# A two-layer graph transformer on one core: layer 1 of a group runs one turn later, and its input is transposed by VectorE blocks and DRAM

## The chip, the core and the metric

The kernel runs on one NeuronCore of a Trainium2 chip. TensorE (PE in the profile, with PEld for its weight loads) multiplies matrices, VectorE (DVE), ScalarE (ACT) and GpSimd (POOL) work on elements, and the queue of SyncE (SP) issues all the large transfers. The metric is the device time of one execution in microseconds. Lower is better.

## The reference

`x` is 64 graphs of 128 nodes with 256 features in fp32, `adj` a 0/1 matrix of 128 x 128 for each graph. Two layers follow one another; a graph needs nothing of another graph.

```
# layer 0 (8 heads of 32)
nx = LN(x); q, k, v = nx@wq+bq, nx@wk+bk, nx@wv+bv
attn = softmax(q k^T / sqrt(32) + (adj > 0 ? 0.1*adj*adj : -inf))
x1 = x + (attn v)@wo + bo
x2 = x1 + gelu(LN(x1)@w1 + b1)@w2 + b2          # hidden 1024
# layer 1 (one head of 256)
s = (x2@Wq)(x2@Wk)^T / sqrt(256), -inf where adj == 0
y = x2 + softmax(s)@(x2@Wv)@Wo + bo1
out = LN(y)*gamma + beta
```

## The kernel before

**Groups and turns.** The 64 graphs are cut into 17 groups: group 0 and group 16 have two graphs, the others four (512 nodes). The work is a software pipeline written out by hand. Each engine has a function `turn` that lists its instructions for several groups in different phases, and turn `gp` is the one in which group `gp` has its Q, K, V and its scores. In that turn group `ga = gp-1` has its attention product, output projection and second LayerNorm, and group `gb = gp-2` has the whole MLP and then all of layer 1. VectorE and GpSimd also finish the last LayerNorm of group `gc = gp-3` and prepare the first one of group `gn = gp+1`. Groups 0 to 3 are started by `first_turn` and `second_turn`; turns 4 to 14 (to 15 on TensorE and ScalarE) are a hardware loop on each engine, the ones after are written out, and `last_turn` drains the pipe. Nothing is scheduled by a tool: the order on an engine is the order of the calls, and semaphores tie the engines together.

**Precision.** A product that needs fp32 accuracy is three passes in a faster format: a high part and a low part of each operand (`mm3`, lines 455 to 457). So each transposed activation has a ScalarE instruction that writes the high part and a VectorE instruction (`..._low`) that writes source minus high part.

**Names.** `mlp_up(g, j)` is one of eight tiles of the hidden layer; it waits for `h_low` of tile j-4, since four PSUM banks are shared. `mlp_down(g, q)` is the second MLP product of a pair of graphs. `residual2` adds it to `x1_b2` (x1 plus the bias b2) and gives `x2`. In layer 1, `t_project` is x2 times the folded Wq Wk^T, `scores1` the scores, `biased1` masks them and takes the row maximum, `exps1` the exponentials, `vo_project` x2 times the folded Wv Wo, `p1_transpose` and `attend1` the product with the probabilities, `residual3` gives `y`. `sums3`, `moments(3)`, `norm3` (VectorE) and `rstd`, `gain`, `offset` (GpSimd, lines 1920, 2004, 2009) are the last LayerNorm. In layer 0, `biased`, `exps`, `inverse`, `normal` and `blocks` make the probabilities of a pair of graphs, and `norm2` normalizes `x1` for the MLP.

**How x2 is transposed.** TensorE multiplies by the identity: `x2_transpose(gb)` (line 724) is eight 128x128 products into banks 4 and 5, `x2T_copy` and `x2T_high` on ScalarE write the fp32 copy and the high part, `x2T_low` on VectorE the low part. They sit in the middle of the turn, behind the second residual of the MLP. The input of layer 0 already takes another way: `xblocks` transposes 32x32 blocks on VectorE, SP stores them to DRAM (`store_nx`, four transfers) and loads them back in another order (`load_nx`), which completes the transpose; `nx_high` and `nxT_low` (line 1429) split what landed. The probabilities take that way too (`blocks`, `store_blocks`, `load_blocks`).

**The mask of layer 1.** GpSimd keeps a float copy of the adjacency one group behind: `move_up` (line 1968) copies `adj_g` to `adj_f`, `mask1` (line 1961) makes the penalty `pen1` of it.

**SP's queue** is one list in order; an issue behind one that waits, waits too.

Of the kernel before, what the change touches and what calls it, by code (L numbers as in the profile page):

```python
# [64 lines left out]
def build(nc, x, adj, ln1_g, ln1_b, ln2_g, ln2_b, wq, bq, wk, bk, wv, bv, wo, bo, w1, b1, w2, b2,  # L65
# [12 lines left out]
    with ExitStack() as ctx:  # L78
# [28 lines left out]
        probe = sb("probe", [128, 1])  # L107
# [6 lines left out]
        adj_f = sb("adj_f", [128, PER, NODES])  # L114
# [43 lines left out]
        parked_x = nc.dram_tensor("parked_x", (KT, 4, 32, NODES // 32, PER, 32), f32).ap()  # L158
        parked_end = nc.dram_tensor("parked_end", (KT, 4, 32, NODES // 32, 2, 32), f32).ap()
# [18 lines left out]

        def nx_split(part, g, t):
            return part[:, t, toks(g)].rearrange("p (b a i) -> p b a i", a=4, b=size(g))  # L180
# [6 lines left out]
        def home(n, g):  # L187
            return (own if is_last(g) else usual)[n]
# [36 lines left out]

        l1_bank, l1_mm_bank = (4, 6, 5), (7, 4)

        def at(n, g):
            if isinstance(g, int) and g < len(first_banks):
                return first_banks[g].get(n, usual_banks[n])  # L230
            return (own_banks if is_last(g) else usual_banks)[n]

# [56 lines left out]
        dve_blocks = sem("dve_blocks")  # L289
        dve_xblocks, nx_store, nx_load, xbo_load = sem("dve_xblocks"), sem("nx_store"), sem("nx_load"), sem("xbo_load")  # L290
# [32 lines left out]
        def _(sp):  # L323
# [38 lines left out]

            def store_blocks(g, q):
# [53 lines left out]
            def turn(gp, gc):  # L417
# [15 lines left out]
            with sp.Fori(3, GROUPS - 4) as g:  # L433
                turn(g + 1, g - 2)
            for g in range(GROUPS - 3, GROUPS):
                turn(g, g - 3)
            store(GROUPS - 3)
            for q in range(2):
                sp.wait_ge(dve_out, 2 * q + 2)
                sp.dma_start(out[graph0(GROUPS - 2) + 2 * q:graph0(GROUPS - 2) + 2 * q + 2].rearrange("b n d -> n b d"),  # L440
                             y[:, of_pair(q), :]).then_inc(out_store, 16)
# [7 lines left out]
        def _(pe):  # L449
# [132 lines left out]
            def project_v(g, q):  # L582
# [7 lines left out]
                elif not (isinstance(g, int) and g < 3):  # L590
                    pe.wait_ge(*((dve_x1, pair0(g) - 1), (dve_vo, g - 2))[q])
# [64 lines left out]
            def n2_transpose(g, B):  # L656
                if B:
                    pe.wait_ge(act_t, g)
                    pe.wait_ge(dve_t, g)
                    pe.wait_ge(dve_s1, g)  # L660
# [7 lines left out]
            def mlp_up(g, j, A):  # L668
# [78 lines left out]
            def vo_project(g, q, P):  # L747
                if isinstance(g, int) and g == 0:
                    pe.wait_ge(dve_lo, SPLIT["vo1"])
                if P and q == 0:  # L750
                    pe.wait_ge(act_v, pair0(g + 2) + 1)
                if P and q == 1:
                    pe.wait_ge(dve_x1, pair0(g + 1) + size(g + 1) // 2)
# [33 lines left out]
            def turn(gp, ga, gb):  # L787
# [9 lines left out]
                mlp_down(gb, 0)  # L797
                mlp_down(gb, 1, (0,))
                if size(gp) > 2:
                    scores(gp, 1)  # L800
                mlp_down(gb, 1, (1,))
# [12 lines left out]
                pe.wait_ge(act_vo, gb + 1)  # L814
                attend1(gb, 0)
                pe.wait_ge(dve_vo, gb)
                if size(gp) > 2:
                    pe.wait_ge(act_v, pair0(gp) + 2)
                attend1(gb, 1)
# [73 lines left out]
            def last_turn(ga, gb):  # L893

                for j in range(4):
                    mlp_up(gb, j, True)
                mlp_up(gb, 4, True)
                attend(ga, 0)
                mlp_up(gb, 5, True)
                mlp_up(gb, 6, True)  # L900
                out_project(ga, 0)
                mlp_up(gb, 7, True)
                mlp_down(gb, 0)
                n2_transpose(ga, False)
                mlp_down(gb, 1)
# [63 lines left out]
            with pe.Fori(3, GROUPS - 2) as g:  # L969
                turn(g + 1, g, g - 1)  # L970
            turn(GROUPS - 1, GROUPS - 2, GROUPS - 3)
            last_turn(GROUPS - 1, GROUPS - 2)


        @block.scalar
        def _(act):
# [111 lines left out]
            def x2T_copy(g, tiles=range(KT)):  # L1088
                for t in tiles:
                    act.wait_ge(pe_x2T, 2 * g + t + 1)  # L1090
                    identity(home("x2T_f", g)[:, t, toks(g)], bank[at("x2", g)[t]][:, toks(g)]).then_inc(act_x2T, 1)

            def x2T_high(g, tiles=range(KT)):
                for t in tiles:
                    act.wait_ge(act_x2T, 2 * g + t + 1)
                    identity(home("x2T", g)[0][:, t, toks(g)], home("x2T_f", g)[:, t, toks(g)]).then_inc(act_x2T_hi, 1)

            def last_x2T(g):

                for t in range(KT):  # L1100
                    act.wait_ge(pe_x2T, 2 * g + t + 1)
# [26 lines left out]
            def turn(gp, ga, gb):  # L1128
                whole = size(gp) > 2
                run(probe[:, :], minus_half[:, 0:1], ACT.Gelu)  # L1130
                nx_high(gp)
                for j in range(4):
# [6 lines left out]
                run(probe[:, :], minus_half[:, 0:1], ACT.Exp)  # L1139
# [6 lines left out]
                if whole:  # L1146
                    exps(gp, 1, 0)
# [999 lines left out]
```

## Time and profile before

| | us |
|---|---|
| time, median of 3 runs (890.16 to 891.61) | 890.98 |
| the profiled execution's own time | 891.15 |
| its span, first to last instruction | 889.4 |
| TensorE busy in the span | 853.3 (96%) |
| VectorE busy | 703.3 (79%) |
| ScalarE busy | 609.6 (69%) |
| GpSimd busy | 507.5 (57%) |
| transfers | 107.32 MB, 121 GB/s |

The span is what the rows below lie in; 1.75 us of the execution's own time lie around it. From turn 5 to turn 14 the turns are alike and one is about 50.9 us long. The time of a row is counted from the start of the span. The steady turn that the rows below show most of is turn 9: it ends where the next turn's first MLP product starts, at 473.44 us.

### The profile page before, as it was taken

The page shows a single profiled execution, that of the slowest core. Times are in us where ns is not written, and L with a number is a line of the kernel's source. Part 1 is how long each engine was busy: PE and PEld are TensorE (multiplying, and loading weights), DVE is VectorE, ACT ScalarE, POOL GpSimd, SP SyncE. Part 2 cuts the span into 40 slices and gives each one's busy share as a digit, 9 for nine tenths or more (in the row PEclk, how much of TensorE's full clock was granted, in tenths as well). Part 3 has the DMA queues.
Part 4 walks back from the last instruction along what each step waited for, and adds up shares of the span by engine and source line. Part 5 has one row for each costly group of instructions (what it writes and reads, how often), then busy time and mean ns, then how long its engine had stood idle before and what let it go on. Part 6 is the DMA issues. An engine that isn't in the chain of part 4 may idle for free.

```text
span 889.4 us, 21938 instructions
## 1 busy us (share of the span) xinstructions
PE 853.3 (96%) x7059; PEld 754.3 (85%) x7059; DVE 703.3 (79%) x2548; ACT 609.6 (69%) x1830; POOL 507.5 (57%) x374
## 2 busy tenths in 40 slices
PE   8899797799999999999999999999999999999996
PEld 8787687589898989889898988989798988989795
DVE  6695777868888898888888797888889887875636
ACT  5684865667868676776768676786867677684542
POOL 3522743756666565775647566666656577655312
PEclk9899999799999999999999999999999999999998
DMA  8000245445536353444546343553635343343001
GB/s 272 16 24 13 66 105 187 129 152 136 177 94 200 101 180 99 127 154 114 181 118 189 106 146 105 138 176 95 200 96 182 86 124 120 99 143 115 24 1 36
DMA packets 131122, 107.32 MB, mean 121 GB/s; under 512 B 5750, under 2 KB 112908, under 8 KB 131084
## 3 DMA queue, kind: packets, MB, share of 16 engines
q1 hardware_dynamic: 131068, 106.85, 40.5%
q8 instruction: 19, 0.31, 0.2%
q14 instruction: 19, 0.16, 0.1%
q10 hardware_dynamic: 16, 0.00, 0.0%
HBM read 61.48 MB, written 45.35 MB: 120 GB/s over the span
## 4 chain that ended last, share of the span: by engine, by line
PE 74%; ACT 3%; DVE 3%; POOL 1%; issue 1%; DVEq 0%; POOLq 0%
PE bank L455 21%; PE bank L457 20%; PE bank L456 20%; PE bank L618 3%; PE bank L743 3%; PE bank L774 3%; PE bank L642 3%; ACT p L1116 2%; PE bank L724 1%; DVE p L1540 1%; PE bank L767 0%; POOL p_s L2013 0%; POOL x_bo L1983 0%; POOL x_b L1993 0%; DVE stats L1375 0%
## 5 line engine op out<-in xcount | busy, mean ns | idle before, releaser
L1052 ACT ACTIVATE p_s<-bank,neg_max 128x128 f32<-128x128 f32 x464 | 163.0, 391 | 78.2 <-DVE neg_max L1443 78.1
L2013 POOL TENSOR_TENSOR p_s<-p_s,rsum 128x512 f32<-128x512 f32 x116 | 118.1, 1041 | 73.9 <-DVE rsum L1450 52.2
L455 PE MATMUL bank<-w_hi,hT_hi 128*128 128x256 f32 x512 | 147.5, 288 | 1.3 <-DVE hT_lo L1316 1.3
L457 PE MATMUL bank<-w_hi,hT_lo 128*128 128x256 f32 x512 | 144.1, 281 | 0.0
L456 PE MATMUL bank<-w_lo,hT_hi 128*128 128x256 f32 x512 | 144.0, 281 | 0.0
L1443 DVE CUSTOM_DVE_ANT_0 bank<-bank,bias 128x128 f32<-128x128 f32 x464 | 117.4, 325 | 2.0 <-PE bank L618 1.5
L455 PE MATMUL bank<-n2T_hi,w_hi 128*128 128x512 f32 (+1 forms) x272 | 111.4, 409 | 5.1 <-DVE hT_lo L1316 5.1
L1083 ACT ACTIVATE bank<-bank,vec_cols 128x512 f32<-128x512 f32 (+1 forms) x136 | 86.5, 636 | 31.1 <-PE bank L457 22.5
L1052 ACT ACTIVATION_READ_ACCUMULATOR p_s<-bank,neg_max 128x1 f32 x464 | 107.1, 231 | 0.0
L456 PE MATMUL bank<-n2T_lo,w_hi 128*128 128x512 f32 (+1 forms) x272 | 105.2, 387 | 0.0
L457 PE MATMUL bank<-n2T_hi,w_lo 128*128 128x512 f32 (+1 forms) x272 | 105.1, 387 | 0.0
L455 PEld LDWEIGHTS bank<-w_hi,hT_hi 128*128 128x128 f32 x512 | 96.3, 188 | 5.4 <-DVE hT_lo L1316 2.3
L1920 POOL TENSOR_TENSOR rstd<-ve,minus_half 128x4 f32<-128x4 f32 (+1 forms) x49 | 50.0, 1020 | 87.3 <-DVE ve L1385 85.8
L456 PEld LDWEIGHTS bank<-w_lo,hT_hi 128*128 128x128 f32 x512 | 96.4, 188 | 0.0
L457 PEld LDWEIGHTS bank<-w_hi,hT_lo 128*128 128x128 f32 x512 | 96.4, 188 | 0.0
L1316 DVE TENSOR_TENSOR hT_lo<-bank,hT_hi 128x512 fp32r<-128x512 f32 (+1 forms) x136 | 84.0, 647 | 10.7 <-ACT hT_hi L982 10.7
L1999 POOL TENSOR_TENSOR x<-x,bo_r 128x1024 f32<-128x1024 f32 (+1 forms) x16 | 37.4, 2338 | 94.8 <-PE bank L724 90.8
L982 ACT ACTIVATE hT_hi<-bank 128x512 fp32r<-128x512 f32 (+1 forms) x136 | 78.1, 574 | 5.3
L1466 DVE STREAM_TRANSPOSE pT<-p_s 128x512 f32<-128x512 f32 x116 | 78.5, 695 | 3.3 <-POOL p_s L2013 2.7
L455 PEld LDWEIGHTS bank<-n2T_hi,w_hi 128*128 128x128 f32 x272 | 52.4, 193 | 22.3 <-DVE hT_lo L1316 12.3
L1443 DVE DVE_READ_ACCUMULATOR2_ANT neg_max<- 128x1 f32 x512 | 68.1, 133 | 0.1
L457 PEld LDWEIGHTS bank<-n2T_hi,w_lo 128*128 128x128 f32 x272 | 52.2, 192 | 11.0
(242 smaller groups left out, 2432.6 us busy)
## 6 DMA issues: line engine op xcount, KB each, us to landing
parked<-pT SPq DMA_DIRECT2D x116, 256.0 KB, 3.8
pT<-parked SPq DMA_DIRECT2D x15, 1024.0 KB, 5.5
p_s<-parked SPq DMA_DIRECT2D x14, 1024.0 KB, 7.7
xs<-in_x SPq DMA_DIRECT2D x15, 512.0 KB, 3.9
out<-y SPq DMA_DIRECT2D x14, 512.0 KB, 3.0
x_bo<-in_x SPq DMA_DIRECT2D x13, 512.0 KB, 3.8
parked_x<-nx SPq DMA_DIRECT2D x48, 128.0 KB, 2.5
hT_hi<-parked_x SPq DMA_DIRECT2D x12, 512.0 KB, 5.0
```

What stands on the lines that cost most here:

```text
L455: mm(out, a_hi, b_hi, start=first, stop=False)
L456: mm(out, a_hi, b_lo, start=False, stop=False)
L457: return mm(out, a_lo, b_hi, start=False, stop=last)
L982: return run(dst, src, ACT.Identity, **kw)
L1052: last = run(to, of, ACT.Exp, scale=-1.0, bias=neg_max[:, r, place:place + 1], accum_out=psum[:, r, place:place + 1])
L1083: run(h, h, ACT.Gelu, bias=cols["b1"][:, j:j + 1]).then_inc(act_h, 1)
L1316: return V.tensor_tensor(dst, src, hi.bitcast(f32), ALU.subtract)
L1443: last = V.tensor_tensor_reduce(scored if by_blocks(g) else p_s[:, r, place, :], scored, bias0[:, 2 * q + place // 2, :], -1.0, -3.0 * MAS ...
L1466: V.transpose(pT[:, r, :, :].rearrange("p b (l i) -> p l b i", l=4), p_s[:, r, :, :].rearrange("p l (b j) -> p l b j", j=32)).then_inc(dve ...
L1920: P.tensor_tensor(t["rstd"][:, 0:k], t["ve"][:, 0:k], minus_half[:, 0:k], ALU.pow).then_inc(ln_pool[n], 1)
L1999: P.tensor_tensor(x[:, 0:k, :], x[:, 0:k, :], row_of("bo1", k), ALU.add).then_inc(pool_x2b, 1)
L2013: P.tensor_tensor(p_s[:, r, :, :], p_s[:, r, :, :], rsum[:, r, :, None].to_broadcast([128, 4, NODES]), ALU.mult).then_inc(pool_p, 1)
```

## The change

Layer 1 of a group moves one turn later, to group `gl = gp-3`, and the last LayerNorm with it, to `gc = gp-4`. This is so for groups 2 to 14 (`late(g)`); groups 0, 1, 15 and 16 keep TensorE's transposes. The parts:

- TensorE: no `x2_transpose` in the turns. Turn 4 has no layer 1 at all (`gl` is None); `last_turn` gets the layer 1 of group 14 between its MLP products.
- VectorE: `x2blocks(gb)` (two block transposes of x2 into `x1_b2`) stands where `x2T_low(gb)` stood; `x2T_low(gl)` now stands behind `norm3(gc)` and reads both its operands from SBUF.
- ScalarE: `landed_high(gl)` (two instructions) ahead of the turn's gelus, and the four instructions of `x2T_copy`/`x2T_high` gone.
- GpSimd: `mask_landed(gb)` makes the mask from an adjacency that is loaded again; `mask1` and `move_up` are gone. `x2_plus_bo(gb)` moves from between the two halves of the probabilities to behind the last of them.
- SP: in each turn four stores of 128 KB and one load of 512 KB for the transpose, a store and a load of 512 KB for x2 itself (it comes back in `y`, to be added in `residual3`), and a load of 256 KB for the adjacency.

The core of the diff:

```
+def late(g):
+    return not (isinstance(g, int) and (g < 2 or g > GROUPS - 3))
 # SP
-            def turn(gp, gc):
+            def turn(gp, gb, gl, gc):
...
                     load_adj(gp + 1)
-                store(gc)
+                load_adj1(gb)
+                if gc is not None:
+                    store(gc)
                 store_blocks(gp, 0)
+                if gl is not None:
+                    load_y(gl)
                 if not is_last(gp):
                     load_nx(gp + 1)
+                store_x2T(gb)
                 load_xbo(gp)
                 if not is_last(gp):
                     store_blocks(gp, 1)
+                load_x2T(gb)
                 for q in pairs(gp):
                     load_blocks(gp, q)
+                store_x2(gb)
 # TensorE
                 mlp_down(gb, 1, (1,))
                 out_project(ga, 0)
-                x2_transpose(gb)
                 out_project(ga, 1)
                 project_v(gp, 0)
-                t_project(gb)
-                vo_project(gb, 0, True)
-                scores1(gb)
-                vo_project(gb, 1, True)
+                t_project(gl)
+                vo_project(gl, 0, True)
+                scores1(gl)
+                vo_project(gl, 1, True)
                 n2_transpose(ga, True)
-                p1_transpose(gb)
+                p1_transpose(gl)
...
+            turn(4, 3, 2, None)
+            with pe.Fori(4, GROUPS - 2) as g:
+                turn(g + 1, g, g - 1, g - 2)
 # VectorE
+            def x2blocks(g):
+                dve.wait_ge(dve_x2, pair0(g) + 2)
+                turned = flat(x1_b2[:, :, :]).rearrange("p (t c b i) -> p t b c i", t=KT, c=4, b=PER)
+                for t in range(KT):
+                    V.transpose(turned[:, t], x2[:, :, 128 * t:128 * t + 128].rearrange(
+                        "p b (c j) -> p b c j", c=4)).then_inc(dve_x2blocks, 1)
...
+                    if late(g):
+                        V.tensor_tensor(nx_split(x2T[1], g, t), x2_landed(g, t), nx_split(x2T[0], g, t).bitcast(f32),
+                                        ALU.subtract).then_inc(dve_x2T, 1)
 # GpSimd
                 pool.wait_ge(ln_dve[2], ln_end(ga))
                 if size(gp) > 2:
                     normal(gp, 1, 3)
+                x2_plus_bo(gb)
                 x_plus_bo(gp)
                 x1_plus_b2(ga)
-                mask1(ga)
-                move_up(gp)
+                mask_landed(gb)
```

How the instructions stand on VectorE between the last LayerNorm and the scores' maxima, in the loop of the steady turns. `y` is the layer-1 output being normalized, `avT_lo` and `n2T_lo` the low parts that the output projection of group `ga` needs. Before:

```order
L1316 TENSOR_TENSOR hT_lo<-bank,hT_hi 128x512
L1392 TENSOR_SCALAR y<-y,mv,rstd 128x256 x4
L1478 REGISTER_ALU
L1316 TENSOR_TENSOR avT_lo<-bank,avT_hi 128x512
L1478 REGISTER_ALU
L1316 TENSOR_TENSOR n2T_lo<-bank,n2T_hi 128x512
```

Now:

```order
L1506 TENSOR_SCALAR y<-y,mv,rstd 128x256 x4
L1651 ISA
L1653 TENSOR_TENSOR x2T_lo<-x2T_f,x2T_hi 128x512
L1651 REGISTER_ALU
L1653 TENSOR_TENSOR x2T_lo<-x2T_f,x2T_hi 128x512
L1592 REGISTER_ALU
L1430 TENSOR_TENSOR avT_lo<-bank,avT_hi 128x512
```

Two instructions with both operands in SBUF have come between the LayerNorm and the low part of the attention output.

The end of GpSimd's steady turn, from the last probabilities (`p_s`) on; `x` is x2, `x_b` is `x1_b2`, `pen` the mask. Before:

```order
L2013 TENSOR_TENSOR p_s<-p_s,rsum 128x512
L1981 REGISTER_ALU
L1983 TENSOR_TENSOR x_bo<-x_bo,bo_r 128x1024
L1987 ISA
L1992 REGISTER_ALU
L1993 TENSOR_TENSOR x_b<-x,b_r 128x1024
L1961 TENSOR_SCALAR pen<-adj_f 128x512
L1968 COPY adj_f<-adj_g 128x512
```

Now:

```order
L2181 TENSOR_TENSOR p_s<-p_s,rsum 128x512
L2167 TENSOR_TENSOR x<-x,bo_r 128x1024
L2146 TENSOR_TENSOR x_bo<-x_bo,bo_r 128x1024
L2158 TENSOR_TENSOR x_b<-x,b_r 128x1024
L2121 CAST pen<-adj_w 128x512
L2124 TENSOR_SCALAR pen<-pen 128x512
```

The addition to x2 has moved in ahead of the three others, and the mask is now last.

## Rows read from the trace of the kernel before

**Rows 1.** Stretches: length, busy per engine, PEclk, DMA share, GB/s; turn 4, steady, last
```profile
160.61:219.07 58.46, 54.47 (x425) 47.52 (x424) 46.25 (x164) 39.04 (x122) 36.68 (x28) 0.92 0.47 135
...
483.63:534.49 50.86, 50.81 (x426) 44.80 (x425) 43.19 (x157) 36.99 (x111) 32.80 (x24) 1.00 0.47 139
...
825.00:876.50 51.50, 50.05 (x375) 45.57 (x374) 26.91 (x71) 25.65 (x57) 12.77 (x9) 1.00 0.03 11
```
**Rows 2.** Timeline, TensorE, second half of turn 9: start, length, what, idle before it
```profile
455.65 0.28 PE L455 MATMUL bank<-wo_hi,avT_hi 128*128 128x256 f32 x1
...
457.07 1.03 PE L724 MATMUL bank<-ident,x 128*128 128x128 f32 x8
457.86 0.36 PE L455 MATMUL bank<-wo_hi,n2T_hi 128*128 128x256 f32 x1
...
460.90 0.50 PE L455 MATMUL bank<-x2T_hi,qk_hi 128*128 128x512 f32 x1
...
463.78 0.28 PE L455 MATMUL bank<-vo_hi,x2T_hi 128*128 128x256 f32 x1
...
465.31 2.02 PE L743 MATMUL bank<-x2T_f,tT 128*128 128x128 f32 x16
...
468.74 1.09 PE L664 MATMUL bank<-ident,nx 128*128 128x128 f32 x8
469.66 0.90 PE L767 MATMUL bank<-ident,p 128*128 128x128 f32 x4
470.31 0.36 PE L455 MATMUL bank<-wv_hi,nxT_hi 128*128 128x256 f32 x1
...
471.81 1.98 PE L774 MATMUL bank<-vo,p1T 128*128 128x256 f32 x8
473.44 0.58 PE L455 MATMUL bank<-n2T_hi,w_hi 128*128 128x512 f32 x1
```
**Rows 3.** The same for VectorE in turn 9
```profile
438.77 1.38 DVE L1392 TENSOR_SCALAR y<-y,mv,rstd 128x256 f32<-128x256 f32 x4 [0.72 <-POOL rstd L1920]
441.73 0.69 DVE L1316 TENSOR_TENSOR avT_lo<-bank,avT_hi 128x512 fp32r<-128x512 f32 x1 [1.58 <-ACT avT_hi L982]
...
452.99 0.30 DVE L1443 CUSTOM_DVE_ANT_0 bank<-bank,bias 128x128 f32<-128x128 f32 x1 [0.15 <-PE bank L618]
...
464.52 0.65 DVE L1533 COPY tT<-bank 128x512 f32<-128x512 f32 x1
...
465.21 1.38 DVE L1392 TENSOR_SCALAR nx<-x,mv,rstd 128x256 f32<-128x256 f32 x4
...
474.67 1.75 DVE L1429 TENSOR_TENSOR nxT_lo<-hT_hi,nxT_hi 128x512 fp32r<-128x512 f32 x2
```
**Rows 4.** The same for ScalarE, end of the first pair's exponentials
```profile
449.73 0.30 ACT L1052 ACTIVATION_READ_ACCUMULATOR p_s<-bank,neg_max 128x1 f32 x1
```
**Rows 5.** The same for GpSimd
```profile
440.23 2.38 POOL L2004 TENSOR_TENSOR y<-y,gamma_r 128x1024 f32<-128x1024 f32 x1 [1.62 <-DVE y L1392]
...
467.75 2.38 POOL L1983 TENSOR_TENSOR x_bo<-x_bo,bo_r 128x1024 f32<-128x1024 f32 x1
...
472.57 1.94 POOL L1961 TENSOR_SCALAR pen<-adj_f 128x512 f32<-128x512 f32 x1
```
**Rows 6.** Timeline of GpSimd in the drain, an addition within SBUF
```profile
839.34 2.38 POOL L2009 TENSOR_TENSOR y<-y,beta_r 128x1024 f32<-128x1024 f32 x1
```
**Rows 7.** Timeline of VectorE at the same time
```profile
840.12 1.63 DVE L1385 TENSOR_SCALAR ve<-mv 128x2 f32<-128x2 f32 x1
```
**Rows 8.** Timeline of GpSimd, last instruction of its turn 10
```profile
525.57 1.17 POOL L1968 COPY adj_f<-adj_g 128x512 f32<-128x512 f32 x1 [0.16 <-issue]
```
**Rows 9.** Timeline of VectorE at the same time
```profile
525.57 1.71 DVE L1429 TENSOR_TENSOR nxT_lo<-hT_hi,nxT_hi 128x512 fp32r<-128x512 f32 x2
```
**Rows 10.** All instructions of line 1968: count, ns min/median/max, first and last start
```profile
L1968 POOL COPY adj_f<-adj_g x17: 397/612/1168, 12.4 to 823.7; 128x512 f32<-128x512 f32 x15, 128x256 f32<-128x256 f32 x2
```
**Rows 11.** Page, costliest groups: count, busy us, mean ns, idle before and releaser
```profile
L1466 DVE STREAM_TRANSPOSE pT<-p_s 128x512 f32<-128x512 f32 x116 | 78.5, 695 | 3.3 <-POOL p_s L2013 2.7
```

More of the change, by code:

```diff
@@ L891, in second_turn, with last_turn @@
                 attend1(1, 1)
-            def last_turn(ga, gb):
-                for j in range(4):
-                    mlp_up(gb, j, True)
+            def last_turn(ga, gb, gl):
+                mlp_up(gb, 0, True)
+                mlp_up(gb, 1, True)
+                t_project(gl)
+                mlp_up(gb, 2, True)
+                mlp_up(gb, 3, True)
+                scores1(gl)
+                vo_project(gl, 0, False)
+                attend(ga, 0)
                 mlp_up(gb, 4, True)
-                attend(ga, 0)
+                vo_project(gl, 1, False)
                 mlp_up(gb, 5, True)
                 mlp_up(gb, 6, True)
+                pe.wait_ge(dve_vo, gl)
                 out_project(ga, 0)
                 mlp_up(gb, 7, True)
+                p1_transpose(gl)
                 mlp_down(gb, 0)
+                attend1_pairs(gl)
+                mlp_down(gb, 1, (0,))
                 n2_transpose(ga, False)
-                mlp_down(gb, 1)
+                mlp_down(gb, 1, (1,))
                 for j in range(4):
@@ L1146, in turn @@
                 if whole:
[L1147 to L1154 removed]
+                    for r in range(HPT):
+                        exps(gp, 1, r)
                 v_copy(gp, 0)
[L1156 to L1158 removed]
+                if gl is not None:
+                    t_copy(gl)
+                    vo_copy(gl)
+                    exps1(gl)
                 n2T_copy(ga)
[L1160 removed]
+                if gl is not None:
+                    p1T_copy(gl)
                 if whole:
@@ L1233, in second_turn, with last_turn @@
                 exps(3, 1, 3)
-            def last_turn(ga, gb):
-                run(probe[:, :], minus_half[:, 0:1], ACT.Gelu)
+            def last_turn(ga, gb, gl):
+                run(probe[:, 0:1], minus_half[:, 0:1], ACT.Gelu)
+                landed_high(gl)
                 gelu(gb, 0)
                 gelu(gb, 1)
-                for j in range(2, 5):
-                    gelu(gb, j)
+                t_copy(gl)
+                gelu(gb, 2)
+                gelu(gb, 3)
+                vo_copy(gl)
                 attn_high(ga, 0)
-                for j in range(5, HT):
-                    gelu(gb, j)
+                gelu(gb, 4)
+                gelu(gb, 5)
+                run(probe[:, 1:2], minus_half[:, 0:1], ACT.Exp)
+                exps1(gl)
+                run(probe[:, 0:1], minus_half[:, 0:1], ACT.Gelu)
+                gelu(gb, 6)
+                gelu(gb, 7)
+                p1T_copy(gl)
                 n2T_copy(ga)
@@ L1630, in turn @@
                 h_low(gb, 7)
-                norm3(gc)
+                if gc is not None:
+                    norm3(gc)
+                if gl is not None:
+                    x2T_low(gl)
                 attn_low(ga, 0)
@@ L1663, in turn @@
                     blocks(gp, 1, 0)
-                t_copy(gb)
+                if gl is not None:
+                    t_copy(gl)
                 if whole:
@@ L1804, in last_turn @@
                 h_low(gb, 1)
+                t_copy(gl)
                 h_low(gb, 2)
+                norm3(gc)
+                h_low(gb, 3)
+                biased1(gl)
                 attn_low(ga, 0)
-                h_low(gb, 3)
-                norm3(gc)
+                vo_copy(gl)
+                h_low(gb, 4)
                 residual1(ga, 0, True)
-                h_low(gb, 4)
+                h_low(gb, 5)
                 sums2(ga, 0)
                 moments(2, ga)
-                h_low(gb, 5)
                 h_low(gb, 6)
@@ L2053, in second_turn @@
                 x1_plus_b2(2)
-                mask1(2)
-                move_up(3)
                 for r in range(HPT):
@@ L2065, in turn @@
                 bias(gp)
-                rstd(3, gc)
-                gain(gc, size(gc))
-                offset(gc, size(gc))
+                if gc is not None:
+                    rstd(3, gc)
+                    gain(gc, size(gc))
+                    offset(gc, size(gc))
                 for r in range(HPT):
                     normal(gp, 0, r)
-                x2_plus_bo(gb)
                 if size(gp) > 2:
@@ L2090, in last_turn @@
                 pool.wait_ge(ln_dve[2], ln_end(ga))
+                mask_landed(gb)
                 x1_plus_b2(ga)
+                rstd(3, gl)
                 x2_plus_bo(gb)
-                mask1(ga)
+                gain(gl, size(gl))
+                offset(gl, size(gl))
+                mask_landed(ga)
                 x2_plus_bo(ga)
```

256 lines of the change are left out of this document (177 added, 79 removed).

## The prediction

> **What bounds the kernel now.** First the chain of work that ended last, whose steps are TensorE's almost throughout. Then the stretches: in a steady turn of 50.86 us TensorE is busy for 50.81, VectorE for 43.19, GpSimd for 32.80 [rows 1]. So a steady turn is TensorE's list of instructions and nothing else; VectorE has 7.7 us left over. Turn 4 is different, 58.46 us with 54.47 busy at a granted clock of 0.92, that is partly at the lower of TensorE's two levels (1.2 instead of 2.4 GHz); the drain from 825.0 to 876.5 us is full again, 50.05 of 51.50 [rows 1]. Last, the timelines of turn 9: where each other engine stands against TensorE [rows 2 to 5].
>
> **What the transposes cost.** The eight stand from 457.07 us to the start of the next product at 457.86, and that one is followed more slowly for another 0.08: 0.87 us [rows 2]. Thirteen groups lose them. One wait of about 0.1 us ahead of `t_project` (460.90) goes too, so a turn that is bounded by TensorE gains 0.95.
>
> **What layer 1 costs, since it moves.** From [rows 2]: `t_project` 460.90 to 463.78, the first `vo_project` to 465.31, `scores1` and the second `vo_project` to 468.74, `p1_transpose` 469.66 to 470.31, `attend1` 471.81 to 473.44. That is 2.88 + 1.53 + 3.43 + 0.65 + 1.63 = 10.1 us of TensorE. Turn 4 loses it, `last_turn` gains it, turns 5 to 16 exchange one group's for another's.
>
> Term 1, the drain. There TensorE has 1.45 us of idle time in 51.5 [rows 1], so 10.1 us of work is nearly 10.1 us of time. The two waits that this idle time is made of do not go: ScalarE must now change its table for `exps1` and back between gelu 5 and gelu 6, which makes the last `h_low` of group 15 late by about as much as the wait that it replaces. **+10.1**, bounds +8.7 (all idle time filled) and +12 (table changes uncovered).
>
> Term 2, turn 4. It has 54.47 - 0.87 - 10.1 = 43.5 us of work left, but the second LayerNorm of group 3 does not come sooner. The end of `norm2` (465.21 + 1.38 = 466.59) is 10.9 us behind the end of the MLP, where the output projection starts (455.65) [rows 2, 3]; without `t_copy` (0.65), and with two block transposes (1.3) for what `x2T_low` and its waits took there (about 2.45), it is 9.1 to 9.3. In steady turns layer 1 fills this gap. In turn 4 only `project_v(gp, 0)` is left for it, 1.4 us, so TensorE stands for about 8 us ahead of `n2_transpose`. The two output projections (457.07 - 455.65 = 1.4 us each), which stood behind the last MLP product, stand before it now and put it off by 2.8. Summed, turn 5's first product comes 2 to 3 us sooner than at 219.07 us. But such an idle time lowers the granted clock (turn 4's 0.92), and the start of turn 5 then waits for VectorE (term 4 below), so at the seventh MLP tile of turn 5 I expect **+0.3**, bounds -3 (clock back soon) and +1. GpSimd's `mask1` and `move_up`, gone ahead of turn 4, save at most 0.9 of this, for the residuals on VectorE end nearly as late.
>
> **The steady turns: what the new places do.** The decisive view is how VectorE and GpSimd share SBUF. GpSimd runs one addition from 839.34 to 841.72; a VectorE instruction on four numbers, issued at 840.12, takes 1.63 us, to 841.75 [rows 6, 7]. At 525.57 both begin, GpSimd's copy and the two `nxT_low`: 1.71 us for the two and 1.17 for a copy whose median is 0.61 [rows 8 to 10]; I read this as VectorE's first, then the copy, then VectorE's second. So an instruction of VectorE with two SBUF operands, or a scaling within SBUF, excludes GpSimd's and waits for its whole length, and the two engines take turns. The low parts that read PSUM (`avT_lo`, 0.69) and the block transposes (mean 695 ns beside GpSimd's `normal`) do not show it [rows 3, 11].
>
> The Trainium skill says the same as a rule (GPSIMD Engine Reference, "1. Specifications"): GpSimd's SBUF interfaces are shared with VectorE, and contention arises with VectorE instructions in a 2-port mode or with two SBUF inputs. By that rule the moved `x2T_low`, which read PSUM before and reads SBUF twice now, speaks against this change; the trace above agrees. The page gives no price, the sum takes it from the rows.
>
> Term 3, `x2T_low` behind `norm3`. `norm3` ends at 440.15, and its end is what `gain` waits for: it starts at 440.23 and takes 2.38 [rows 3, 5]. VectorE's first half (0.6) gets in ahead, to 440.7; then `gain`, to 443.1; then the second half, to 443.7. `avT_lo`, which could start at 441.73, starts 1.9 us later, `n2T_lo` and `biased` (16 maxima) behind it about 1.7. ScalarE's exponentials of the first pair end at 450.03 [rows 4], now 451.75, and the second pair's scores on TensorE, at 451.59 before, wait 0.3. Behind them on VectorE stand the last `inverse`, `residual2`, three `blocks`, then the second `biased`: 454.55 instead of 452.99 [rows 3]. From there VectorE has no gap: the old order reached `t_copy`'s end at 465.17 [rows 3] with 2.45 for `x2T_low`; now 465.17 + 1.56 - 2.45 + 1.3 = 465.6. `scores1` waits for it: 465.7 instead of 465.31 [rows 2], though TensorE could be there at 464.6. That wait eats the transposes' gain. `norm2` ends 0.4 late, `biased1` and `exps1` 0.1 late, `attend1` ends 0.14 us later than before: **-0.95 turned into +0.14** per turn.
>
> Term 4, the start of the next turn. GpSimd goes on after `norm2` (467.05 now): `normal` 1.04, then three additions of 2.38 (before: two, from 467.75 [rows 5]), to 475.35; then the cast, like the copy 0.61 [rows 10], and the mask, 1.94 [rows 5]. `residual3` ends at 474.85, so `nxT_low` waits 0.5 for the last addition, then once more for the cast: 2.3 us for 1.75 [rows 3]. The small scaling ahead of `rstd` ends as the mask does, at 479.1. So `h_low` 0 to 3 come 0.6 to 0.75 later against `attend1`, and `h_low(3)` is what `mlp_up(7)` waits for already. **+0.6** per turn. ScalarE's 1.14 us for `landed_high` is hidden: it is busy for 36.99 of 50.86 us [rows 1], and `h_low(0)` waits for VectorE's own list, not for it. Bounds of terms 3 and 4 together: -0.95 (no collision costs anything) and +1.3 per turn.
>
> SP's queue. The stores of `store_x2T` (some 2 us of issuing) stand ahead of `load_xbo`, which is needed 6 us later; `load_x2T` stands ahead of `load_blocks`, which lands about 2 us later with 4 to 5 in hand. 0, and +1 per turn if that reserve is gone. The added 2.25 MB per turn of 51 us are 44 GB/s on 139 [rows 1].
>
> **The sum.** From turn 5's seventh tile to turn 15's are ten turns of +0.74: +7.4. Turn 16 has half of VectorE's work, so it keeps TensorE's gain: -0.95 + 0.14 = -0.8. With term 1, +10.1, and term 2, +0.3: +17.0 us on the profiled execution's 891.15, 908.2. It lies 0.17 above the median of the runs, so I forecast **908.0**, with its own range 901 to 915.
>
> **Rivals.**
> A. The engines do not collide there: VectorE's second half gets in ahead of `gain`, or the exclusion is shorter. Then the turns stay TensorE's: 10 x -0.8 (0.15 left for `nxT_low`) or -0.95, -0.95 in turn 16, +10.1 in the drain, -1.7 in turn 4 (clock back sooner). 891.15 - 9.5 - 0.95 + 10.1 - 1.7 = 889.1, or 891 with the smaller values. For it: VectorE's 7.7 spare us. Against: [rows 6 to 10]. It decides if `biased` starts no more than 0.8 us late. This is the case on the other side.
> B. `x2T_low` is late, but the second half of the turn takes it up, and each turn comes out even: 891.15 + 0 - 0.95 + 10.1 + 0.3 = 900.6.
> C. GpSimd's `gain` gets in first and `offset` before VectorE's second half: `biased` 2.4 us later still, 10 turns: 908 + 24 = 932. Against: `gain` waits for a semaphore of `norm3`, VectorE's next instruction does not. Or a transfer comes late, +1 per turn: 918.
>
> **Chances.** Forecast 0.62, A 0.17, B 0.12, C and beyond 0.09. A gain needs A with its better values (half of it), and a small rest: faster by over 0.2% (below 889.2) 0.09; within 0.2%, about what this measurement can tell from no change, 0.09; slower 0.82. The range takes in the upper part of A, B and the forecast's own bounds: 890 to 916.
>
> **What the changed profile would show.** Right: TensorE's busy share falls in steady turns and the turn grows to about 51.6; `scores1` is waited for by `tT`; the second `x2T_lo` of each turn takes some 3 us against 0.6 for the first; ScalarE waits longer for `neg_max`; an idle time of about 8 us ahead of `n2_transpose` near 205 us; the drain has layer 1 of group 14 with TensorE full. Wrong: two `x2T_lo` in 1.4 us, a turn of 50 us, or a turn 4 shorter by more than 5 us.

## The result, and the profile after

The changed kernel takes 929.84 us (927.9 to 931.08) against 891.22 before (890.16 to 891.61): ratio 1.0435, 95% interval 1.0422 to 1.0448. It is slower by 38.6 us where 17 were forecast, and outside the range (890 to 916). The profiled execution took 927.9 us, its span is 926.1.

The chain of waits of the page after, by engine and then by line, says at once that something new is in the path:

```profile
PE 61%; DVE 12%; DMA 8%; ACT 5%; issue 5%; SPq 4%; POOL 3%; DVEq 0%; POOLq 0%; ACTq 0%
PE bank L519 17%; PE bank L521 16%; PE bank L520 16%; DMA x2T_f<-parked_x2T 7%; SPq L418 4%; PE bank L708 3%; PE bank L684 3%; PE bank L824 3%; DVE pT L1580 2%; ACT bank L1183 1%; DVE hT_lo L1430 1%; DVE p L1668 1%; ACT hT_hi L1082 1%; ACT x2T_hi L1082 1%; DVE bank L1557 1%
```

New in it are a transfer, `x2T_f<-parked_x2T`, which is what `load_x2T` brings, and SP's line 418, which is `store_blocks`. Now the stretches, as in [rows 1] (length, busy per engine, granted clock, DMA share, GB/s). They are cut where the `attend1` of a turn ends. First the kernel before, from the end of turn 3: turns 4 and 5, turns 6 to 15, turn 16, `last_turn`.

```profile
160.70:270.31 109.61, 105.57 (x850) 92.57 (x849) 89.80 (x320) 76.29 (x233) 69.16 (x51) 0.96 0.47 137
270.31:779.03 508.72, 507.91 (x4241) 448.04 (x4241) 429.34 (x1555) 369.79 (x1111) 326.67 (x231) 1.00 0.46 136
779.03:825.32 46.29, 45.03 (x381) 41.03 (x381) 30.37 (x102) 29.47 (x80) 23.99 (x20) 1.00 0.38 121
825.32:889.40 64.08, 55.02 (x402) 49.15 (x401) 36.03 (x101) 27.33 (x63) 15.35 (x11) 0.96 0.06 21
```

And after, with turns 9 and 10 apart at the end:

```profile
157.59:267.81 110.22, 96.86 (x769) 85.03 (x769) 83.83 (x295) 70.00 (x217) 60.81 (x45) 0.92 0.55 161
267.81:800.67 532.86, 506.89 (x4161) 444.50 (x4161) 445.04 (x1575) 354.59 (x1091) 333.10 (x231) 0.98 0.60 174
800.67:850.71 50.04, 45.78 (x373) 41.13 (x373) 31.45 (x104) 28.39 (x80) 26.56 (x21) 0.97 0.57 165
850.71:926.10 75.39, 66.02 (x467) 59.69 (x465) 42.56 (x131) 33.96 (x79) 25.05 (x18) 0.95 0.14 47
428.15:481.88 53.73, 51.09 (x417) 44.95 (x417) 44.73 (x159) 35.53 (x110) 33.31 (x24) 0.97 0.60 176
481.88:534.51 52.63, 50.09 (x418) 43.68 (x417) 44.76 (x159) 35.32 (x110) 33.35 (x24) 1.00 0.62 179
```

Of the 36.7 us between the spans, +0.6 are in turns 4 and 5, +24.1 in turns 6 to 15, +3.8 in turn 16 and +11.3 in the drain; -3.1 lie ahead of turn 4. The last can't be put down to the change: over the eleven profiled kernels that share the changed kernel's code up to there that stretch ends anywhere from 157.2 to 160.7 us, and over the two with the code of before at 160.7 and 161.5. How much of it is scatter stays open, which is why turns are compared here and not starts.

So the drain is near the forecast and the steady turn is not: 53.3 us in the mean, not 51.6. In each turn TensorE has one large wait, of 2.3 to 2.7 us in turns 6 to 15. The start of turn 10 shows where it is from: first TensorE's `scores1`, the last reader of the old `x2T_f`, then SP's queue, ScalarE, VectorE with one line of GpSimd, and TensorE's fifth MLP tile (start, length, what, idle before it and who ended it).

```profile
473.46 1.95 PE L824 MATMUL bank<-x2T_f,tT 128*128 128x128 f32 x16
```

```profile
469.02 1.90 SPq L397 DMA_DIRECT2D parked_x2T<-x_b  x4
471.19 0.41 SPq L373 DMA_DIRECT2D x_bo<-in_x  x1
478.41 2.82 SPq L418 DMA_DIRECT2D parked<-pT  x4
481.48 0.92 SPq L404 DMA_DIRECT2D x2T_f<-parked_x2T  x1
```

```profile
482.12 1.14 ACT L1082 ACTIVATE nxT_hi<-hT_hi 128x512 fp32r<-128x512 f32 x2
486.58 1.15 ACT L1082 ACTIVATE x2T_hi<-x2T_f 128x512 fp32r<-128x512 f32 x2 [3.32 <-DMA x2T_f<-parked_x2T]
487.64 0.65 ACT L1183 ACTIVATE bank<-bank,vec_cols 128x512 f32<-128x512 f32 x1
488.40 0.60 ACT L1082 ACTIVATE hT_hi<-bank 128x512 fp32r<-128x512 f32 x1
```

```profile
477.69 0.69 DVE L1580 STREAM_TRANSPOSE pT<-p_s 128x512 f32<-128x512 f32 x1
...
482.76 0.60 POOL L2121 CAST pen<-adj_w 128x512 f32<-128x512 int32 x1
482.77 2.16 DVE L1543 TENSOR_TENSOR nxT_lo<-hT_hi,nxT_hi 128x512 fp32r<-128x512 f32 x2
...
489.03 0.69 DVE L1430 TENSOR_TENSOR hT_lo<-bank,hT_hi 128x512 fp32r<-128x512 f32 x1 [2.06 <-ACT hT_hi L1082]
```

```profile
489.78 0.50 PE L519 MATMUL bank<-n2T_hi,w_hi 128*128 128x512 f32 x1 [2.32 <-DVE hT_lo L1430]
```

The x2 blocks are stored at 469 to 471, `scores1` has read the old `x2T_f` at 475.41, and from then on the new one could be loaded. But `load_x2T` stands in SP's queue behind `store_blocks(gp, 1)`, which waits for VectorE's last block of the second pair (477.69 + 0.69 = 478.38) and then issues for 2.8 us. The load goes out at 481.48 and lands at 486.58. ScalarE has stood in `landed_high` since 483.26, ahead of all eight gelus; TensorE's fifth MLP tile waits for the first `h_low`. It happens in twelve turns: ScalarE waits 41.8 us in all, 3.3 to 3.7 in each of turns 6 to 15.

The collision that the forecast rests on is in the trace too, but the other way round. VectorE (first fence), then GpSimd:

```profile
502.08 1.29 DVE L1653 TENSOR_TENSOR x2T_lo<-x2T_f,x2T_hi 128x512 fp32r<-128x512 f32 x2
503.70 0.69 DVE L1430 TENSOR_TENSOR avT_lo<-bank,avT_hi 128x512 fp32r<-128x512 f32 x1 [0.33 <-ACT avT_hi L1082]
```

```profile
502.25 3.35 POOL L2172 TENSOR_TENSOR y<-y,gamma_r 128x1024 f32<-128x1024 f32 x1 [1.61 <-DVE y L1506]
```

Both halves of `x2T_low` get in (1.29 us for two), and it is `gain` that takes 3.35 us instead of the 2.38 of [rows 5]. It is so in the whole kernel: the median of the fifteen `gain` is 3.36 us here and 2.38 in experiment 2 below, where `x2T_low` stands elsewhere. VectorE loses nothing.

### The profile page after: what moved, and what is told of

Its sections match the earlier page's. It is cut to its first block, busy times and chain, and to the rows that moved or that the text cites. A ratio compares the mean times of both kernels' runs of the same rounds, so it can differ in the third digit from the quotient of the medians.

```text
span 926.1 us, 21993 instructions
## 1 busy us (share of the span) xinstructions
PE 852.5 (92%) x6955; PEld 751.5 (81%) x6955; DVE 720.5 (78%) x2574; ACT 593.7 (64%) x1808; POOL 517.2 (56%) x374
## 4 chain that ended last, share of the span: by engine, by line
PE 61%; DVE 12%; DMA 8%; ACT 5%; issue 5%; SPq 4%; POOL 3%; DVEq 0%; POOLq 0%; ACTq 0%
PE bank L519 17%; PE bank L521 16%; PE bank L520 16%; DMA x2T_f<-parked_x2T 7%; SPq L418 4%; PE bank L708 3%; PE bank L684 3%; PE bank L824 3%; DVE pT L1580 2%; ACT bank L1183 1%; DVE hT_lo L1430 1%; DVE p L1668 1%; ACT hT_hi L1082 1%; ACT x2T_hi L1082 1%; DVE bank L1557 1%
## 5 line engine op out<-in xcount | busy, mean ns | idle before, releaser
L519 PE MATMUL bank<-n2T_hi,w_hi 128*128 128x512 f32 (+1 forms) x272 | 116.0, 426 | 35.8 <-DVE hT_lo L1430 35.2
L1152 ACT ACTIVATION_READ_ACCUMULATOR p_s<-bank,neg_max 128x1 f32 x464 | 110.7, 239 | 0.0
L521 PE MATMUL bank<-n2T_hi,w_lo 128*128 128x512 f32 (+1 forms) x272 | 110.1, 405 | 0.0
L520 PE MATMUL bank<-n2T_lo,w_hi 128*128 128x512 f32 (+1 forms) x272 | 109.9, 404 | 0.0
L519 PEld LDWEIGHTS bank<-n2T_hi,w_hi 128*128 128x128 f32 x272 | 55.3, 203 | 56.8 <-DVE hT_lo L1430 45.8
L1557 DVE DVE_READ_ACCUMULATOR2_ANT neg_max<- 128x1 f32 x512 | 72.3, 141 | 0.1
L521 PEld LDWEIGHTS bank<-n2T_hi,w_lo 128*128 128x128 f32 x272 | 55.0, 202 | 12.0
L520 PEld LDWEIGHTS bank<-n2T_lo,w_hi 128*128 128x128 f32 x272 | 55.3, 203 | 10.8
```

Source lines behind the costliest of these rows:

```text
L519: mm(out, a_hi, b_hi, start=first, stop=False)
L520: mm(out, a_hi, b_lo, start=False, stop=False)
L521: return mm(out, a_lo, b_hi, start=False, stop=last)
L1152: last = run(to, of, ACT.Exp, scale=-1.0, bias=neg_max[:, r, place:place + 1], accum_out=psum[:, r, place:place + 1])
L1557: last = V.tensor_tensor_reduce(scored if by_blocks(g) else p_s[:, r, place, :], scored, bias0[:, 2 * q + place // 2, :], -1.0, -3.0 * MAS ...
```

## The experiments

Theory Q says that the load's place in the queue makes the loss of the steady turns, theory C that it is the collisions. All ratios are against the kernel before, run beside (889.3 to 889.8 us there).

**1. The load one place earlier.**

```diff
                 load_xbo(gp)
+                load_x2T(gb)
                 if not is_last(gp):
                     store_blocks(gp, 1)
-                load_x2T(gb)
```

> Edit: on SP, load_x2T stands ahead of store_blocks(gp, 1) instead of behind it, nothing else. In the changed kernel the load is issued at 481.48 us in turn 9, 3.1 us behind the end of the last block of the second pair (478.38), though its own two conditions hold from about 475.4 us; it lands at 486.58, and ScalarE, which stands in landed_high ahead of the gelus, waits 3.3 to 3.7 us for it in each of twelve turns. Theory Q (queue): the load's place in SP's queue makes nearly the whole loss of the steady turns. Then the load is issued at about 475.5, lands before ScalarE gets there, the wait of TensorE for hT_lo (2.3 to 2.7 us a turn) is mostly gone, a turn takes 50.6 to 51.2 instead of 53.3 us, the kernel 895 to 906 us. Theory C (collisions, my own of the prediction): VectorE and GpSimd in each other's way at x2T_low and nxT_low make the loss; then the turn stays above 52.5 and the kernel above 918 us.

Measured 889.1 us, ratio 0.9992 (0.9982 to 1.0003): 40 us from two lines that change places, and level with the kernel before. Its stretches, as above, and its turn 9 alone:

```profile
158.32:267.12 108.80, 96.02 (x770) 84.50 (x769) 84.00 (x294) 69.47 (x215) 60.49 (x45) 0.93 0.55 167
267.12:767.00 499.88, 497.19 (x4162) 437.66 (x4161) 444.89 (x1575) 354.36 (x1091) 333.05 (x231) 1.00 0.61 186
767.00:812.14 45.14, 43.88 (x374) 40.03 (x373) 31.32 (x104) 28.34 (x80) 26.59 (x21) 1.00 0.57 172
812.14:885.90 73.76, 64.50 (x466) 58.12 (x465) 42.59 (x131) 33.85 (x79) 25.00 (x18) 0.97 0.14 48
417.27:467.32 50.05, 49.77 (x418) 43.73 (x417) 44.69 (x159) 35.44 (x110) 33.33 (x24) 1.00 0.62 189
```

A turn of 50.0, and a time below what theory Q gave too (895 to 906). Turns 6 to 15 are 33.0 us shorter than after: 23.3 of it is TensorE's idle time (25.97 to 2.69, length less busy), and 9.7 its busy time for the same number of instructions, 506.89 to 497.19. The waits also cost clock: of the changed kernel's turns one, 53.73 long, has a granted clock of 0.97, the next, 52.63, has 1.00. In the first, the clock is at its lower level behind the wait of 2.55 us that ends at 436.30:

```profile
438.00:440.00 2.00, 2.00 (x6) 1.58 (x5) 2.00 (x6) 1.94 (x4) 0.72 (x2) 0.50 1.03 393
```

In the second, behind 2.32 us, it is not. Six of the ten turns have such a stretch. SP now issues the load at 461.00 us in the turn that ends at 467.3, and nobody waits for it:

```profile
461.00 0.41 SPq L404 DMA_DIRECT2D x2T_f<-parked_x2T  x1
463.86 2.83 SPq L418 DMA_DIRECT2D parked<-pT  x4
```

**2. ScalarE and VectorE take x2T later; the queue is left.** `landed_high(gl)` goes behind `attn_high`, `x2T_low(gl)` behind the first pair's sixteen `biased`.

> Edit: on ScalarE landed_high stands behind attn_high and ahead of exps, no longer ahead of the gelus; on VectorE x2T_low stands behind the sixteen maxima of the first pair instead of ahead of attn_low. SP's queue is that of the changed kernel, so the load lands as late as there, at a time when nobody waits for it. Theory Q: the same gain as with the load moved, since only the waiting ScalarE carries the late landing to TensorE: 895 to 906 us, 1.2 us of landed_high now ahead of the exponentials, which the wait of 1.8 us there for neg_max covers. Theory C: x2T_low leaves the stretch in which GpSimd has gain and offset; so this too would gain, but only what is lost there, at most 1.5 us a turn: 910 to 922 us. If the landing itself mattered (the transfer's load on the DMA engines), no gain: 928.

Measured 891.43, ratio 1.0018 (1.0006 to 1.0031), again below what Q gave. The load is as late as in the changed kernel and costs nothing: experiment 3, with the load early as well, takes the same time. It is the wait in front of the gelus, not the transfer's load on the DMA engines.

**3. Both.**

> Edit: both of the other two: the load ahead of store_blocks(gp, 1), landed_high behind attn_high, x2T_low behind the first pair's maxima. Theory Q: the two remove the same wait once, so the gains do not add: within 5 us of the better of the two, 893 to 904 us. Theory C: what the first leaves of the collision of x2T_low with gain goes here, so it is faster than the first by 0.7 to 1.5 us a turn, 8 to 15 us.

Measured 891.73, ratio 1.0016 (1.0005 to 1.0028). The two gains do not add, as theory Q says. With `x2T_low` away from `gain`, theory C wanted 8 to 15 us more than experiment 1 gave; its turns are 50.33 us, longer by 0.3 than those of experiment 1. No run shows where these 0.3 come from.

**4. The load later still,** behind `load_blocks`.

> Edit: on SP, load_x2T stands behind load_blocks, that is later than in the changed kernel by two issues and by load_blocks' wait for its stores (some 3 to 4 us); nothing else. Theory Q: ScalarE waits longer by as much, 6 to 7.5 us a turn instead of 3.3 to 3.7, and the turn grows by 2.5 to 4 us: 955 to 975 us. Theory C: the landing isn't what bounds the turn: less than 5 us more, 928 to 935.

Measured 1041.2, ratio 1.1692 (1.1669 to 1.1716). The direction is Q's, the size is 66 us beyond its upper end:

```profile
479.03 1.15 ACT L1082 ACTIVATE x2T_hi<-x2T_f 128x512 fp32r<-128x512 f32 x2 [12.09 <-DMA x2T_f<-parked_x2T]
```

ScalarE waits 12 us. The load is issued at 469.46 and lands 9.6 us later, not 5: it is now behind the two loads (of 1024 KB in the page's list) that `load_blocks` has just started. TensorE waits 10.6 to 11.6 us in a steady turn, and its clock over a turn falls to 0.89 (63.45 us, busy for 52.06).

**5. GpSimd's `x_plus_bo` to where GpSimd waits,** on top of experiment 1 (from turn 5 on, and at the start of `last_turn`). In the turn:

```diff
                 for r in range(HPT):
                     normal(gp, 0, r)
+                if gc is not None:
+                    x_plus_bo(ga)
...
                 x2_plus_bo(gb)
-                x_plus_bo(gp)
                 x1_plus_b2(ga)
                 mask_landed(gb)
```

> Base: the kernel with load_x2T first (889.1 us, turn 50.06, in each turn TensorE waits 0.2 us for the first h_low). Edit on top of it: GpSimd's x_plus_bo goes from the end of the turn to the next turn, between the normals of the two pairs, where GpSimd waits for ScalarE's exponentials anyway. It takes 2.4 us of GpSimd's work out of the stretch in which VectorE has nxT_low (2.1 us for the two there, 1.37 where GpSimd is quiet). Theory E (the exclusion is real, but small): nxT_low takes 1.4 to 1.8 us, the 0.2 us wait goes and turn 5 starts up to 1 us sooner: 885.5 to 888. Theory N (VectorE's order, not GpSimd, sets the first h_low): no change, 889 +- 0.8. Against both: residual1 now waits for x_plus_bo, which shows as a longer turn.

Measured 881.03, ratio 0.9907 (0.9890 to 0.9924), 8 us less than experiment 1 and twice what theory E allowed. By the profiles 6.2 us of it lie in turns 6 to 15 and 2.6 in turns 4 and 5. All instructions of `nxT_low` (count, shortest/median/longest in ns), in the changed kernel and in this one:

```profile
L1543 DVE TENSOR_TENSOR nxT_lo<-hT_hi,nxT_hi x26: 410/1094/1856, 163.6 to 802.3; 128x512 fp32r<-128x512 f32 x24, 128x256 fp32r<-128x256 f32 x2
```

```profile
L1543 DVE TENSOR_TENSOR nxT_lo<-hT_hi,nxT_hi x26: 411/684/1036, 163.6 to 759.0; 128x512 fp32r<-128x512 f32 x24, 128x256 fp32r<-128x256 f32 x2
```

The exclusion costs VectorE something here: 0.41 us for each of two. In the changed kernel `nxT_low` begins 0.01 us behind GpSimd's cast (482.76) and is long; here cast and mask have begun 2.4 us sooner. It moves TensorE's eight MLP tiles by more than the 0.2 us of waiting that the view showed. The first MLP product, the first key product and the next turn's first MLP product, before (the third is in [rows 2]), in experiment 1 and here:

```profile
422.54 0.58 PE L455 MATMUL bank<-n2T_hi,w_hi 128*128 128x512 f32 x1
...
434.17 0.40 PE L455 MATMUL bank<-nxT_hi,wk_hi 128*128 128x512 f32 x1
```

```profile
416.92 0.58 PE L519 MATMUL bank<-n2T_hi,w_hi 128*128 128x512 f32 x1
...
428.96 0.39 PE L519 MATMUL bank<-nxT_hi,wk_hi 128*128 128x512 f32 x1
...
466.97 0.58 PE L519 MATMUL bank<-n2T_hi,w_hi 128*128 128x512 f32 x1
```

```profile
461.23 0.58 PE L519 MATMUL bank<-n2T_hi,w_hi 128*128 128x512 f32 x1
...
472.61 0.39 PE L519 MATMUL bank<-nxT_hi,wk_hi 128*128 128x512 f32 x1
...
510.63 0.58 PE L519 MATMUL bank<-n2T_hi,w_hi 128*128 128x512 f32 x1
```

The tiles take 11.63 us before, 12.04 in experiment 1, 11.38 here. Within a tile the matmuls start every 0.23 or 0.24 us; in experiment 1 three of these steps are 0.34 and one is 0.59, of which the view gives only 0.20 as a wait. The rest of the turn takes 39.27, 38.01 and 38.02. TensorE is now full: in turns 6 to 15 it is busy for 492.75 of 493.70 us, at a clock of 1.00.

**6. `h_low` 0 to 2 first.** VectorE has `h_low` 0 and 1 ahead of `sums1` and `moments`, 2 ahead of `norm1`; ScalarE has `landed_high` behind gelu 3.

> Base as in the one before. Edit on top of it: VectorE has h_low 0 and 1 directly behind nxT_low and ahead of sums1 and moments, h_low 2 ahead of norm1; ScalarE has landed_high behind gelu 3 instead of ahead of gelu 0. TensorE's fifth MLP tile waits for h_low 0: 0.2 us in steady turns, 3.1 at the start of turn 4, 3.0 at the start of turn 5. If VectorE's list sets that wait, the steady turns lose it (50.06 to 49.85) and the starts of turns 4 and 5 lose 1 to 2.5 us each: 882 to 886. If h_low 0 to 3 were late for GpSimd's sake, or norm1, now later, is what the next thing waits for, there is no gain or a loss: 889 to 893.

Measured 905.24, ratio 1.0178 (1.0161 to 1.0195), a loss of 16 us against experiment 1. VectorE, then TensorE at the eighth tile:

```profile
537.61 1.38 DVE L1506 TENSOR_SCALAR xs<-xs,mv,rstd 128x256 f32<-128x256 f32 x4 [0.66 <-POOL rstd L2070]
539.12 1.30 DVE L1536 STREAM_TRANSPOSE nx<-xs 128x512 f32<-128x512 f32 x2
540.35 1.25 DVE L1430 TENSOR_TENSOR hT_lo<-bank,hT_hi 128x512 fp32r<-128x512 f32 x2
```

```profile
541.06 0.50 PE L519 MATMUL bank<-n2T_hi,w_hi 128*128 128x512 f32 x1 [1.85 <-DVE hT_lo L1430]
```

The fourth `h_low`, still behind `norm1` and `xblocks`, is what the eighth tile waits for; the first tiles had been served at its cost. ScalarE's part of the edit is not what makes it late: the fourth `hT_hi` ends at 536.35, and `landed_high` stands behind it.

**7. Turn 4's order.** `residual1`, sums and `norm2` of group 3 ahead of `residual2(gb, 1)`, on top of experiment 1.

> Base as in the first. Edit on top of it: in turn 4 alone, which has no layer 1, VectorE does residual1, the sums and norm2 of group 3 as soon as the output projections are there, ahead of residual2(gb, 1), and GpSimd has rstd(2) ahead of the second pair's normals. TensorE stands 2.6 and 4.1 us there, ahead of project_v and of n2_transpose, for norm2's chain. If that chain is late because of VectorE's order, norm2 ends at about 204 instead of 209 us and turn 4 is 3 to 5 us shorter; x2T lands somewhat later against it and gives back up to 1.5 at the start of turn 5: 884.5 to 887.5. If the chain is late because of its own length (10 us from the end of the MLP), less than 1 us: 888.5.

Measured 888.8, ratio 0.9989 (0.9975 to 1.0003): by the medians nothing. In the profiles turns 4 and 5 are 106.6 us long against 108.8 in experiment 1, which the times do not show. `n2_transpose` comes sooner, but then turn 5 waits for `n2T_low`, left behind the last blocks:

```profile
213.70 0.79 PE L519 MATMUL bank<-n2T_hi,w_hi 128*128 128x512 f32 x1 [3.79 <-DVE n2T_lo L1430]
```

**8. All four.**

> All four edits together: load_x2T first, x_plus_bo later, h_low first with landed_high behind gelu 3, turn 4's order. The three gains lie in different places (the steady wait of 0.2 us, the starts of turns 4 and 5, the two waits in turn 4), except that x_plus_bo and h_low work on the same 0.2 us. Sum of the three expectations less that overlap: -7 to -11 us from 889.1, so 878 to 882 us, 1.0 to 1.3% below the kernel before. If the start of turn 5 is then set by the landing of x2T_f, at most -7: 882 to 884.

Measured 903.44, ratio 1.0161 (1.0146 to 1.0175): experiment 6 rules it, with the same wait of 1.85 us in each turn. My sum had counted a gain that was never measured.

**9. A version that beats both.** Experiments 1 and 5; in turn 4 alone the order of 7, with `x2blocks` ahead of `norm2`, `n2T_low` ahead of the last three blocks, and `h_low` 0 to 3 ahead of `norm1`.

> Base: load_x2T first and x_plus_bo later (881.0 us, turn 49.39 with TensorE full). Edit on top of it, in turn 4 alone: VectorE has h_low 0 to 3 ahead of norm1 and xblocks (moving only 0 to 2 made the fourth late, behind xblocks: 1.85 us a turn); then residual1, sums2 and moments of group 3 ahead of residual2(gb, 1), x2blocks, norm2, and n2T_low ahead of the last three blocks (behind them it cost 3.8 us of waiting at the start of turn 5 in the run before). If turn 4's waits (3.1, 2.6, 4.1 and 1.5 us) are VectorE's order, 3 to 6 us go: 875 to 878. If the landing of x2T_f, or the second LayerNorm's own length, sets the start of turn 5, less than 2 us: 879 to 881.

Measured 878.48, ratio 0.9872 (0.9857 to 0.9887), 1.3% below the kernel before:

```profile
160.21:263.98 103.77, 93.62 (x769) 81.94 (x769) 82.93 (x295) 69.64 (x217) 60.49 (x46) 0.95 0.59 176
263.98:757.64 493.66, 492.74 (x4161) 439.08 (x4161) 436.29 (x1575) 352.89 (x1091) 330.93 (x231) 1.00 0.62 188
```

Turns 4 and 5 are 2.4 us shorter than in experiment 5 (106.18), the steady turns the same (493.66 and 493.70).

**10. The same POOL edit in the kernel before.** `x_plus_bo` between the first pair's normals and `x2_plus_bo`.

> Edit of the kernel before, not of the changed one: GpSimd's x_plus_bo stands between the normals of the first pair and x2_plus_bo, no longer at the end of the turn. There nxT_low (1.75 us for two) meets only move_up (0.6 us). If the exclusion is what makes 1.75 of 1.37, and TensorE's MLP stretch follows it, the turn goes from 50.88 to 50.6 to 50.75: 886.5 to 888.5 us against 889.7. So little of the gain that the same edit brings in the changed kernel (8.1 us) belongs to the edit alone: the rest is the cost of the three additions and the mask that the change puts behind one another there. Rival: the edit gains by itself as much in both, 881 to 883.

Measured 886.24, ratio 0.9964 (0.9951 to 0.9978): 3 us, a turn of 50.58. By difference, 5 of the 8 us of experiment 5 repay what the change itself put in `nxT_low`'s way. What the change is worth with this edit in both kernels, and with the load moved, is 881.0 against 886.2.

**11. The POOL edit without the queue's.**

> Edit of the changed kernel: x_plus_bo later, but load_x2T still behind store_blocks(gp, 1). If the late landing covers the collision, VectorE's nxT_low is done sooner but h_low 0 still waits for ScalarE, which waits for x2T_f: the second pair's blocks set the issue of the load, and they are no earlier, so 926 to 931 us, no change against 928 to 930. If the two costs add (collision and landing on the same path), 920 to 923.

Measured 928.93, ratio 1.0456 (1.0440 to 1.0473), no change. ScalarE still waits 42.1 us in twelve turns; the late landing covers the collision whole.

## Why the prediction was wrong, by its own steps

- **SP's queue: "0, and +1 per turn if that reserve is gone".** This is the step that failed and made the loss. It asked what `load_x2T` holds up behind it (`load_blocks`), and not what it stands behind. With the sentence that `landed_high` is hidden, since "`h_low(0)` waits for VectorE's own list, not for it", it left out the longest chain of the turn: last block, stores, load, landing, gelu. Measured in its place: 3.3 to 3.7 us of waiting on ScalarE per turn, and by experiment 1 33.0 us over turns 6 to 15 and 4.9 in turn 16 (forecast -0.8, measured +3.8, without the late load -1.2). Both ends of the wait stood in the trace of before (fences below). SP's issues of the second pair end at 473.16. The like load of that trace, `load_nx`, which is also 512 KB directly behind four block stores, lands 5.0 us after its issue, so this one would land at about 478.2. ScalarE is free at 475.16: a wait of 3 us.

```profile
470.33 2.83 SPq L366 DMA_DIRECT2D parked<-pT  x4
```

```profile
hT_hi<-parked_x SPq DMA_DIRECT2D x12, 512.0 KB, 5.0
```

```profile
474.02 1.14 ACT L982 ACTIVATE nxT_hi<-hT_hi 128x512 fp32r<-128x512 f32 x2
```

- **Term 3, the collision at `x2T_low`: +1.09 per turn.** This step failed too. VectorE's second half gets in ahead of `gain`, and the two `x2T_lo` take 1.29 us, which the prediction had named as a sign of being wrong. The exclusion is there, but GpSimd paid it (`gain` 3.35 for 2.38 us), and there was slack. So without the late load the forecast of 908.0 would still have been 19 us too high against the 889.1 of experiment 1: for its ten turns of +0.74 that one has -8.8 us in all. Behind the MLP tiles a steady turn takes 38.01 us in experiment 1, 39.27 before: -1.26. That is the transposes' 0.87 and wait of 0.1, and 0.3 that lie in `t_project` (2.78 for 2.88), the first `vo_project` (1.44 for 1.53) and `p1_transpose` (0.56 for 0.65). Why these are shorter no run shows. ([rows 7] has an instruction on 128x2 elements, not on four numbers; the reading doesn't hang on it.)
- **Term 4, `nxT_low`: +0.6 per turn.** Right in place and near in size: the MLP tiles took 12.04 for 11.63 us, +0.41, and experiment 5 takes it away. In the changed kernel it was hidden under the late landing (experiment 11). By the Trainium skill (GPSIMD Engine Reference, "1. Specifications") both places should collide, and both do. In these traces the one that began first kept its time: the cast, 0.01 us ahead of `nxT_low`, took its 0.60, and `nxT_low` went from 0.68 to 1.09 us each; `x2T_low`, 0.17 us ahead of `gain`, lost nothing. The addition that the prediction set ahead of the cast as a wait of 0.5 us was over as `nxT_low` began and cost nothing.
- **Term 1, the drain: +10.1.** Measured +11.3 after and +9.7 in experiment 1, at granted clocks of 0.95 and 0.97 against 0.96.
- **Term 2, turn 4: +0.3.** At the seventh tile of turn 5, counted from the first of turn 4, it is +1.8 after, and +0.7 without the late load. Turn 5's first product comes 3.2 us sooner, where 2 to 3 were said. TensorE stands 2.6 and 4.1 us ahead of `project_v` and `n2_transpose`, 6.6 where 8 were said.
- **Rival A** (889.1 us) has the number of experiment 1 to the tenth, in part by luck: its turn, -0.8 to -0.95, is made of -1.26 and +0.41. Its reason, that VectorE's second half gets in ahead of `gain`, holds. The changed kernel itself is near the 932 of rival C, but by its second reason, the late transfer, which was priced at +1 per turn and cost +3.3 (experiment 1 against the changed kernel).

## What to carry to other kernels

A DMA issue has a place in its queue, and everything ahead of it in that queue is part of its latency: for each moved or added load write down what it stands behind, when that is released, and who waits at the landing. A load that is ready goes ahead of a store that still waits. A stall on TensorE can be paid twice, as idle time and as clock behind it; and before an engine's order is rearranged so that the first of a row of results comes sooner, look at the last of the row.

## What the runs showed of the hardware

- The same 512 KB load lands 3.6 us after its issue (median of 13) when the last issue ahead of it is some 4 us old (experiment 1), 5.1 directly behind four block stores of 256 KB each (the changed kernel), and 9.5 behind two loads of 1024 KB (experiment 4).
- TensorE's waits of 2.3 to 2.7 us in a turn of 53 cost another 9.7 us of slower matmuls in ten turns (506.89 against 497.19 us busy, granted clock 0.98 against 1.00). Behind six of the ten waits the clock is at its lower level for a while, behind the other four it is not. With waits of 10.6 to 11.6 us the granted clock over a turn is 0.89 (experiment 4).
- Where VectorE and GpSimd exclude each other, either one can be the one that waits, and its instruction shows as long, not as waiting: `gain` 3.36 for 2.38 us, `nxT_low` 1.09 for 0.68. Not each overlap costs: in experiment 5 two `nxT_low` begin 0.4 us before the mask's recorded end and take 1.29 us, the mask its 1.94.
- Against the 11.38 us that the eight MLP tiles take without a gap (experiment 5), the kernel before lost 0.25 us and experiment 1 0.66, of which the view shows nothing and 0.20 as waits, in turns whose TensorE looked over 99% busy.
